# Streaming only the used coefficient columns in the scatter products of a graph layer's edge loop

## What is computed

```python
xn  = layernorm(x)
# per edge: r = unit vector of edge_attr; h0 = hidden scalars from xn[src] and r
act = softmax([leaky_relu(h0) @ lsc, 0 ... 0])        # 64 scores, 192 zeros
msg = act * tensor_product(h0, h1, r)                 # 256 values an edge
x   = x + (xn + segment_sum(msg, dst)) + head_mix(xn)
x   = x + top2_experts(layernorm(x))                  # 8 experts, 256 -> 1024 -> 256, exact gelu
```

## Time and profile before

| | us |
|---|---|
| median of 3 runs | 1286.27 (1279.44 to 1294.23) |
| the profiled execution | 1295.63 |
| its span, first to last instruction | 1293.7 |
| mean granted TensorE clock | 0.921 |

### The profile page before, as it was taken

The page is one execution under the profiler, slowest core; times in us unless marked ns, Lnnn a source line. Parts: engine busy times, 40 slices in busy tenths (PEclk is TensorE's granted clock), DMA queues, the critical chain, the costliest instruction groups (busy, mean ns, idle before and its releaser), DMA issues.

```text
span 1293.7 us, 26994 instructions
## 1 busy us (share of the span) xinstructions
PE 1114.3 (86%) x8025; PEld 1052.4 (81%) x8026; DVE 770.7 (60%) x1946; ACT 626.2 (48%) x1945; POOL 657.7 (51%) x726
## 2 busy tenths in 40 slices
PE   1457888888898988889888889879999999999996
PEld 1447878888898888788788889659999999999995
DVE  6957767677777777777777856582333333333331
ACT  3238434344444444444444457515656565656552
POOL 2762665656566566566666413072454454444442
PEclk9578988889889888989898999889999999999998
DMA  8331322323222322232322203437522222222221
GB/s 215 101 93 38 91 82 78 91 83 89 85 87 84 89 85 85 81 89 84 86 82 82 63 2 101 134 140 284 163 41 40 33 36 36 36 36 32 41 33 21
DMA packets 46321, 105.19 MB, mean 81 GB/s; under 512 B 13637, under 2 KB 24438, under 8 KB 44102
## 3 DMA queue, kind: packets, MB, share of 16 engines
q0 software_dynamic: 30720, 69.24, 21.5%
q1 hardware_dynamic: 15558, 35.42, 8.6%
HBM read 87.68 MB, written 16.94 MB: 81 GB/s over the span
## 4 chain that ended last, share of the span: by engine, by line
PE 77%; issue 7%; DVE 6%; ACT 3%; another core or an unknown queue 2%; DMA 1%; POOL 1%; SPq 1%; DVEq 1%; POOLq 0%; ACTq 0%
PE ps L855 21%; PE ps L1020 16%; PE ps L1034 15%; PE ps L783 8%; PE ps L768 4%; PE ps L832 4%; PE ps L815 2%; PE ps L906 1%; PE ps L902 1%; ACT e L1175 1%; PE ps L1004 1%; DMA attr_raw<-in_edge_attr 1%; PE ps L931 1%; POOL free_hot L632 1%
## 5 line engine op out<-in xcount | busy, mean ns | idle before, releaser
L563 POOL DMA_INDIRECT xg<-xn_rows,idx_st x416 | 422.4, 1015 | 302.3 <-issue 107.0
L855 PE MATMUL ps<-sel,xg 128*128 128x120 f32 x2496 | 327.9, 287 | 26.2 <-issue 25.4
L855 PEld LDWEIGHTS ps<-sel,xg 128*128 128x128 f32 x2496 | 314.0, 204 | 32.5 <-issue 31.6
L1020 PEld LDWEIGHTS ps<-xst,w_st 128*128 128x128 f32 x1792 | 211.0, 194 | 5.0 <-issue 2.2
L1020 PE MATMUL ps<-xst,w_st 128*128 128x128 f32 x1792 | 211.5, 277 | 1.7 <-ACT ht_sb L1331 1.1
L1331 ACT ACTIVATE ht_sb<-ps,b_cur 128x128 f32<-128x128 f32 x448 | 127.8, 368 | 168.2 <-PE ps L1020 168.2
L1034 PE MATMUL ps<-w_sb,ht_sb 128*128 x896 | 202.8, 379 | 0.8 <-DVE y_sb L1906 0.8
L668 POOL DMA_INDIRECT out<-y_sb,put_st x56 | 107.5, 1919 | 166.5 <-DVE y_sb L1909 144.2
L1034 PEld LDWEIGHTS ps<-w_sb,ht_sb 128*128 128x128 f32 x896 | 166.4, 191 | 21.4 <-issue 1.2
L783 PE MATMUL ps<-w_f,zt 128*128 128x128 f32 x832 | 133.0, 299 | 32.1 <-issue 31.9
L1175 ACT ACTIVATE e<-ps,neg_top 128x65 f32<-128x65 f32 x416 | 125.7, 326 | 54.3 <-DVE neg_top L1509 45.6
(11 more groups left out here) (294 smaller groups left out, 1445.6 us busy)
## 6 DMA issues: line engine op xcount, KB each, us to landing
w_sb<-in_L_ffn_W SPq DMA_DIRECT2D x16, 1024.0 KB
xg<-xn_rows,idx_st POOLq DMA_INDIRECT x416
x_sb<-in_x SPq DMA_DIRECT2D x5, 560.0 KB
xn_rows<-xn_sb SPq DMA_DIRECT2D x5, 560.0 KB
xn_t<-xn_rows SPq DMA_DIRECT2D x25, 112.0 KB
expert_in_rows<-xf_sb SPq DMA_DIRECT2D x12, 224.0 KB
out<-x_sb SPq DMA_DIRECT2D x12, 224.0 KB
b_bc<-in_L_ffn_b SPq DMA_DIRECT2D x1, 1024.0 KB, 4.5
```

Source lines behind the costliest of these rows:

```text
L563: pool.indirect_dma_start(xg[:, s, tt, M:M + D], None, xn_dram, bass.IndirectOffsetOnAxis(ap=idx_st[:, s, tt:tt + 1], axis=0)).then_inc(ma ...
L855: mm = pe.matmul(ps3[:, s, col:col + n], xg[:, r, tt, lhs0:lhs0 + 128], sel[:, s, lo:lo + n], start=(tt == 0), stop=(tt == TG - 1))
L1020: mm = pe.matmul(h_of(c), w1_st[:, s, kc, c, :], xst[:, s, kc, :], start=(kc == 0), stop=(kc == 1))
```

## The change

The three product sets get their own widths: 40 columns for the coefficient w, 120 for r0 w, r1 w and r2 w, 80 for w and 1/norm, in the order 128, 0, 256 of their weights as before. The first set now begins at coefficient 3 in place of 1. The results lie at columns 0, 40 and 160 of the PSUM bank, 240 in all, and line 1614 adds columns 0 to 240. No product reads beyond the five coefficients, so the padding, its memset, its semaphore and PE's wait for it go. The number of products, of weight loads and of loop semaphores stays.

```diff
-        sel = sb(loop, "sel", [128, 2, (TG * 5 + 1) * WIN])
+        sel = sb(loop, "sel", [128, 2, TG * 5 * WIN])
...
             def scatter_mm(s, r):
-                n = 3 * WIN
-                for col, lhs0, coef0 in ((0, 128, 1), (n, 0, 0), (2 * n, 256, 3)):
+                for lhs0, coef0, n, col in ((128, 3, WIN, 0), (0, 0, 3 * WIN, WIN), (256, 3, 2 * WIN, 4 * WIN)):
                     for tt in range(TG):
                         lo = (tt * 5 + coef0) * WIN
                         mm = pe.matmul(ps3[:, s, col:col + n], xg[:, r, tt, lhs0:lhs0 + 128], sel[:, s, lo:lo + n],
                                        start=(tt == 0), stop=(tt == TG - 1))
                 return mm
-            pe.wait_ge(sel_padded, 1)
...
-                return dve.tensor_tensor(sel[:, s, 0:TG * 5 * WIN].rearrange("p (t k w) -> p t k w", t=TG, k=5),
+                return dve.tensor_tensor(sel[:, s, :].rearrange("p (t k w) -> p t k w", t=TG, k=5),
...
-                return dve.tensor_tensor(win, win, ps3[:, s, 2 * WIN:8 * WIN].rearrange("p (k w) -> p k w", w=WIN), ALU.add)
+                return dve.tensor_tensor(win, win, ps3[:, s, 0:6 * WIN].rearrange("p (k w) -> p k w", w=WIN), ALU.add)
...
-            dve.memset(sel[:, :, TG * 5 * WIN:], 0.0).then_inc(sel_padded, 1)
```

More of the change, by code:

```diff
@@ L319, in gps_layer_kernel @@
         head_ready, head_used = ([sem(f"{n}{k}") for k in (0, 1)] for n in ("head_ready", "head_used"))
-        kv_ready, sel_padded = sem("kv_ready"), sem("sel_padded")
+        kv_ready = sem("kv_ready")
         class GroupSems:
```

## The result

The changed kernel takes 1303.58 us (median of 4 runs, 1297.22 to 1305.84) beside 1282.86 us for the kernel before (4 runs, 1279.14 to 1294.23): a ratio of 1.012, 95% interval 1.0082 to 1.0157. In a later set of runs, in which the kernel before takes 1294.62 us, the same pair gave 1317.6 us, ratio 1.0203 (1.0135 to 1.0271). One of those four runs of the changed kernel, 1327.73 us, counts as slow; without it their median is 1314.78 us. So the change makes the kernel slower, by some 20 us in both sets. The forecast was 35 us, 1321 us: 2.7% where 1.2% was measured, about twice too much.

What follows compares the result with a forecast made beforehand. The prediction took PE to bound the edge loop, with DVE close behind. 0 (memset) + 0 (pace) + 35 us (clock) on the median 1286.27 us gave 1321 us, 2.7% slower; 8 in 10 range 1281 to 1345 us.

Steps and rivals of the forecast that it cites:

- The pace at full clock: Scatter products in the edge loop: narrower ones follow each other no faster; 0 taken, between 0 and 0.40 us a group.
- the one-column row: Line 978: 20 one-column products, each with a 128-column weight load, 0.111 us apart, as with 120 columns; so no gain.
- The memset: One DVE instruction of 125 ns at 78.2 us and PE's wait for it go: at most 0.1 us, 0 taken.
- The clock: Edge loop: a narrower scatter keeps PE longer at the lower clock, 54 to 87 us more; 35 us lost; chance 0.52.
- the fall behind the one-column products: Behind line 978's products the clock stands at 0.50 though weight loads were busy 2.31 of 3.80 us; support for the clock step.
- 11 stretches that go on longer: Low stretches with at least 8 scatter instructions in their last 3.4 us, each 3.4 to 4.8 us longer: 37 to 53 us.
- five new ones: Five stalls that the full clock survived may each become a low stretch of 3.4 to 6.8 us: 17 to 34 us.
- The price of the clock: Edge loop: PE is the bound at the lower clock, so half the added low time is lost: 27 to 44 us, 35 taken.
- PE's idle time on "issue" about as before: Sign in the profile after: PE's waits on issue in the loop, 31.1 + 25.4 + 20.1 us at three lines, stay.
- clock unchanged: Rival: weight loads count for the clock, or stalls alone decide it, so 0 us: 1286 us; chance 0.32.
- Faster: Rival: the loop's pace follows the columns; a group falls from 4.67 to 4.27 us, 42 us in all: 1244 us; chance 0.06.
- Far slower: Rival: the narrow scatter holds the lower clock for several groups; low stretches double, 116 us more, 58 us lost: 1344; chance 0.10.

Runs made afterwards that it cites:

- the fifth round: Changed kernel's order and addresses, 25 stalls of PE put in, at 2880, 1920 and 960 columns a group: 1348.32, 1389.64 and 1441.59 us.
- paused_cols120: Changed kernel's order and addresses, but 120 columns in every product (2880 a group), with 25 stalls of PE put in: 1348.32 us.
- paused_after_b: Changed kernel (1920 columns a group) with the same 25 stalls of PE put in: 1389.64 us.
- the second round: 25 stalls of PE put in by held row DMAs: kernel before 1435.83 us, changed kernel 1465.85 us; the pair without them again, ratio 1.0203.
- wide_160_b: Changed kernel's layout with 160 columns in all three product sets and the padding back, against the kernel before: 1184.45 us, ratio 1.0321.

## Why the prediction was right in its direction and wrong in its size

*The pace at full clock* was right: 0 forecast, 2.63 against 2.67 us a scatter measured, some 4 us in 104 groups at most. The formula of the Trainium skill ("TensorE: Matmul & The Clock Gate", section "Back-to-back issue gap") gave an estimate of 42 us of gain. The section says itself that it is for an isolated product and that in a stream of weight loads and products both set the spacing; this scatter is such a stream. The 24 instructions of 40, 120 and 80 columns take 2.63 us, 0.110 us each, and show no such gain, and the one-column row told so beforehand. *The memset* was right at 0.

*The clock* was right in place and mechanism. Forecast 71 us more at the lower level and a mean clock of 0.86; measured 76 and 63 us more in the two pairs, and 0.86. The forecast said that the clock would come back only behind the scatter; the timeline at 291.92 us shows it. Its weakest support, the fall behind the one-column products, is replaced by the fifth round. That the amount fits is partly luck. It was made of 37 to 53 us for 11 stretches that go on longer and 17 to 34 us for five new ones. No stretch came on top (23 and 22 before, 22 and 21 after), and the longer ones brought all of it: the mean stretch went from 5.1 to 8.8 us in the first pair. The first term was too small, and the second measured nothing.

*The price of the clock*, "so half of it is lost", was somewhat too high. I took half of the added low time, 35 us. The table gives 31.1 us more paced work for 76.4 us of it in the first pair and 23.0 for 63.3 in the second. Not all of the added low time meets a working PE: some of it lies on the stalls, where it costs nothing. In the fifth round the lower clock grew by 110.6 us from paused_cols120 to paused_after_b, and PE was busy in 89 us of that; paced work grew from 542.4 to 583.0, by 40.6 us, not 55.

*The step that failed* is the price of the clock together with the condition it rests on, the sentence "PE's idle time on 'issue' about as before": the added low time was to reach the end at one half, with nothing given back elsewhere. In the profiles most of the miss lies in that condition. The idle time fell by 18.7 and 15.4 us in the two pairs, as the sum of distances shows, by 11.1 and 16.1 us in the waits at the three lines. In the first pair of profiles: 31.1 of work, less 18.7 of idle time, less 4.2 for a scatter that began earlier (107.2 in place of 111.4 us), and 2.0 behind the loop, is 10.2 us, the difference of the spans 1303.9 and 1293.7. How much of this is the kernel's and how much these single executions' is less sure: they differ by 10.2 and 5.8 us, the medians by 20.7 and 23.0. So up to 10 and 17 us of the fall can belong to the executions that were profiled, and in the second pair that could be all of it. What doesn't hang on them is the sum: in the second pair all executions together had 75 us more at the lower clock and 22 us more time, where a price of one half with nothing given back asks for 37. So about 15 us less was lost than the forecast's rule gives; how they divide between low time that costs nothing and idle time given back stays open.

Whether the idle time falls *because* PE is slower is not settled. For it: both pairs of profiles show it, and the episodes of stalls (starts of products over 0.45 us apart, counted as one within 9 us) are 27 or 28 in each profile before and 24 or 25 in each after, by where the count begins. Stalls of a fixed length gave nothing back (240.2 to 238.7, and 173.6 to 172.2 us), which fits as well. Against a firm verdict: the single executions above, and that the kernel that would have told, PE slowed at full clock by 160 columns, met no stalls in three rounds. What the stalls come from is open too; in the profile PE waits there for nothing that it shows.

*The rival "clock unchanged"* turned out to be true where PE doesn't stall: 1.0005, and there the change is neutral. I had taken the stalls for a fixed part of the kernel. *"Faster"* found nothing for it. *"Far slower"* needed a doubling of the low time (116 us more), and the stalls put in in the second round brought even more (133 us, yet 30 us of time): its price of one half had the same fault.

The range, 1281 to 1345 us, holds the measured time; the 1321 in it does not describe it.

## What to carry to other kernels

Narrowing a streamed operand saves nothing where narrow and wide products follow each other at the same step, as 1 to 120 columns do here (0.111 us); look for the row with the narrowest product before you expect a gain. It can cost: a PE that comes out of a stall at the lower clock works it off sooner with wide products than with narrow ones, so before columns are taken away, look at whether the kernel has stalls and what runs right behind them. And price time at the lower clock by the work that PE issues in it, not by half of its length. Where two kernels are explained by one profile each, check that the profiled executions differ as the medians do; here they didn't.

## What the runs showed of the hardware

- The same kernel took 1147 to 1148 us in four rounds and 1283 to 1295 us in the other two sets of runs. The profiles place the difference in PE's waits on issue (0.8 to 0.9 us in the loop there, 77 to 78 us at three lines here) and in what goes with them (0 to 5 us at the lower clock in the loop there, 117 us here). What brings the stalls is open. A comparison of two kernels can come out differently by it, here 1.0005 and 1.012 to 1.020.
- With everything else equal, 2880, 1920 and 960 columns a group gave 171, 281 and 377 us at the lower clock. All weight loads were the same, and PE was busy for 500 to 510 of 660 us in each, so neither explains the difference.
- At full clock, f32 instructions with a weight load each follow each other in 0.136 us with 160 columns (wide_160_b), and in 0.111 us with 120 columns and with one.
